# Graph attention: what the scan waits for, and the order of widening, exponentials, node maxima and compares

## The reference

```
s = einsum(Qh, Kh) / sqrt(HEAD_DIM)                 # one score for a node and head, 8 heads
alpha = leaky_relu(s[src] + s[dst], 0.2)            # edges, with a loop of each node to itself
m = segment_max(alpha, dst)
e = exp(alpha - m[dst])
a = e / segment_sum(e, dst)[dst]
attn = segment_sum(Vh[src] * a, dst)                # 256 values for a node
h = x + (attn @ Wo + bo)
```

## Time and profile before

| | |
|---|---|
| median of 3 runs | 4592.16 us (4591.9 to 4592.49) |
| the profiled execution | 4596.53 us, span 4594.5 us |
| busy share of the span: PE, DVE, ACT, POOL | 79%, 45%, 27%, 57% |
| mean granted TensorE clock | 0.891 |
| attention stage | from about 620 to 1800 us of the span |

### The profile page before, as it was taken

One profiled execution on the slowest core, in us unless ns is written; L12 is line 12 of the kernel. 1 busy time (PEld: TensorE's weight loads), 2 busy tenths in 40 slices (PEclk: granted clock), 3 DMA queues, 4 the chain that ended last, 5 costly groups with the idle time before them and its releaser, 6 DMA issues. The chain is left out here.

```text
span 4594.5 us, 70306 instructions
## 1 busy us (share of the span) xinstructions
PE 3626.4 (79%) x16651; PEld 2353.7 (51%) x16652; DVE 2077.2 (45%) x7633; ACT 1232.0 (27%) x2424; POOL 2630.5 (57%) x2830
## 2 busy tenths in 40 slices
PE   3877746666666667975999998788888888588998
PEld 1223335555555555864777776343343343367776
DVE  6976657777777775354222221222222222333332
ACT  3973322222222222254333333000000000122222
POOL 4001166666666663023666664777777777477775
PEclk9999967777777777975999999899999999799999
DMA  4431133333333331046888876777777777666675
GB/s 150 168 139 51 49 98 103 103 106 104 103 103 103 106 104 50 0 116 188 239 244 245 248 234 184 217 225 230 226 226 230 226 226 229 176 203 205 201 211 167
DMA packets 352403, 750.64 MB, mean 163 GB/s; under 512 B 82289, under 2 KB 161183, under 8 KB 348872
## 3 DMA queue, kind: packets, MB, share of 16 engines
q0 software_dynamic: 208336, 538.34, 41.3%
q10 hardware_dynamic: 72332, 112.04, 7.7%
q1 hardware_dynamic: 71529, 98.27, 6.5%
HBM read 654.57 MB, written 93.84 MB: 163 GB/s over the span
## 5 line engine op out<-in xcount | busy, mean ns | idle before, releaser
L1695 POOL DMA_INDIRECT l_gathered<-table,record x850 | 818.7, 963 | 399.5 <-issue 277.3
L780 POOL DMA_INDIRECT a_gathered<-table,record x850 | 812.3, 956 | 386.5 <-issue 263.9
L2055 POOL DMA_INDIRECT l_gathered<-table,record x850 | 814.4, 958 | 302.0 <-issue 296.2
L2149 PE MATMUL bank<-l_gathered,l_onehot 128*125 128x512 f32 x1700 | 811.2, 628 | 161.7 <-DMA l_gathered<-table,record 161.4
L2149 PEld LDWEIGHTS bank<-l_gathered,l_onehot 128*125 128x125 f32 x1700 | 325.2, 197 | 620.9 <-issue 357.4
L1110 PE MATMUL bank<-a_gathered,a_onehot 128*125 128x264 f32 x1700 | 517.9, 458 | 111.1 <-DVE a_gathered L908 111.1
L1825 ACT ACTIVATE l_part<-l_packed 128x1000 fp32r<-128x1000 bf16 (+1 forms) x300 | 314.2, 1072 | 530.1 <-PE bank L1906 427.6
L1110 PEld LDWEIGHTS bank<-a_gathered,a_onehot 128*125 128x125 f32 x1700 | 357.2, 221 | 193.1 <-DVE a_gathered L908 67.1
L1925 PE MATMUL bank<-l_gathered,l_onehot 128*125 128x256 f32 (+1 forms) x1275 | 329.3, 415 | 86.0 <-DMA l_gathered<-table,record 86.0
L2088 DVE SCALAR_TENSOR_TENSOR l_z<-l_own,one_eps,bank 125x512 f32<-125x512 f32 x50 | 37.3, 747 | 707.3 <-PE bank L2156 707.3
L1906 PE MATMUL bank<-rows_first,l_part 125*125 125x512 f32 x1250 | 307.5, 405 | 28.6 <-ACT l_part L1825 28.6
(11 more groups left out here) (265 smaller groups left out, 5042.4 us busy)
## 6 DMA issues: line engine op xcount, KB each, us to landing
l_packed<-adjacency ACTq DMA_DIRECT2D x200, 250.0 KB, 4.9
adjacency<-d_stage SPq DMA_DIRECT2D x25, 1562.5 KB
l_packed<-adjacency ACTq DMA_DIRECT2D x100, 281.2 KB, 5.8
l_gathered<-table,record POOLq DMA_INDIRECT x1700, 3.7
a_gathered<-table,record POOLq DMA_INDIRECT x850
table<-rows_first POOLq DMA_DIRECT2D x50, 250.0 KB, 3.3
table<-l_work ACTq DMA_DIRECT2D x50, 250.0 KB
l_own<-table SPq DMA_DIRECT2D x50, 250.0 KB
```

The lines of the kernel that those rows point to most:

```text
L780: pool.indirect_dma_start(out=gathered0[s][:, j * TW:(j + 1) * TW], out_offset=None, in_=table0, in_offset=bass.IndirectOffsetOnAxis(ap=re ...
L1695: pool.indirect_dma_start(out=gathered[g][:, j, :], out_offset=None, in_=table, in_offset=bass.IndirectOffsetOnAxis(ap=record[k.t][:, j, 0 ...
L2055: pool.indirect_dma_start(out=gathered[s][:, j * w:(j + 1) * w], out_offset=None, in_=table, in_offset=bass.IndirectOffsetOnAxis(ap=record ...
L2149: last = pe.matmul(sum_ps[s][0:NB, 0:w], onehot[s][:, j, :], rows[:, j, :], start=False, stop=(j == T - 1), skip_group_check=True)
```

## The change

The scan no longer waits for `prepared` but for a semaphore of its own, set by the reset row (`reset_ready`). On ACT the widening of a block's one-hot moves from the end of the round before into the block's own round, behind the self exponential. The exponential that goes to PSUM, for which DVE waits, comes first of three activations; the one that goes into the gathered rows comes second, with a semaphore (`sums_weighed`) for which PE waits ahead of quarter 0; the copy of the node maxima comes last. On DVE the next block's compares move behind the block's node maxima.

```diff
@@ vector @@
                     r = count_of(dve, rounds[s])
                     rows = gathered0[s].rearrange("p (j c) -> p j c", c=TW)
-                    dve.wait_ge(prepared[s], r)
+                    dve.wait_ge(reset_ready[s], r)
                     dve.wait_ge(rows_gathered[s], r * GATHERED)
...
                     if after is not None:
                         prepare_small(after[0], 2 * after[1] + after[0])
-                        prepare_onehot(after[0])
                     dve.wait_ge(block_begun[s], i + 1)
                     node_maxima(s, 2 * i + s, r)
+                    if after is not None:
+                        prepare_onehot(after[0])
                     if before is not None:
                         attend(before[0])
@@ scalar @@
-                    act.activation(reset[s][:, :, 1:T], rec[:, 1:T, 2].unsqueeze(1).broadcast_to([P, HEADS, T - 1]), ACT.Copy)
+                    act.activation(reset[s][:, :, 1:T], rec[:, 1:T, 2].unsqueeze(1).broadcast_to([P, HEADS, T - 1]),
+                                   ACT.Copy).then_inc(reset_ready[s], 1)
...
-                    act.activation(run_m[s][:, :], node_m[s][:, :], ACT.Copy)
-                    act.activation(rows[:, :, D:TW], alpha2[s][:, :, :], ACT.Exp)
                     act.activation(node_ps[s][:, FACTOR:FACTOR + T * HEADS].rearrange("p (j h) -> p j h", h=HEADS), alpha2[s][:, :, :],
                                    ACT.Exp).then_inc(weights_ready[s], 1)
+                    act.activation(rows[:, :, D:TW], alpha2[s][:, :, :], ACT.Exp).then_inc(sums_weighed[s], 1)
+                    act.activation(run_m[s][:, :], node_m[s][:, :], ACT.Copy)
...
                     if before is not None:
                         self_exp(*before)
+                    widen(s)
                     begin_block(s, i)
...
                     if before is not None:
                         copy_attended(*before)
-                    if after is not None:
-                        widen(after[0])
@@ tensor @@
                     if q == 0:
                         pe.wait_ge(onehot_wide[s], r)
+                        pe.wait_ge(sums_weighed[s], r)
                         pe.wait_ge(block_done[s], i + 1)
```

More of the change, by code:

```diff
@@ L667, in build @@
                                                                       pair("weights_ready"))
-            weighted, block_begun = pair("weighted"), pair("block_begun")
+            weighted, block_begun, reset_ready, sums_weighed = (pair("weighted"), pair("block_begun"), pair("reset_ready"),
+                                                               pair("sums_weighed"))
             self_loaded, self_shifted, self_weight = pair("self_loaded"), pair("self_shifted"), pair("self_weight")
@@ L1088, in _ @@
                 prepare(0)
-                widen(0)
                 over_blocks(act, first_round, more_rounds)
```

## The result

The changed kernel takes 4574.96 us (median of 6 runs, 4572.1 to 4579.97) against 4592.61 of the kernel before: a ratio of 0.996 [0.9947, 0.9973]. It is faster, as forecast, but it gains 17.6 us, where 56.6 were forecast. It lies inside the range by 1 us (the range ended at 4576), in the part that the prediction gave to the partial case of the rival "no change".

A forecast was written before the change was run, and what follows sets the result against it. Bound: a loop of waits between engines in the attention stage, none full. Gains of 48 x 0.95 + 50 x 0.32 = 61.6 us, less 5 for the clock, gave 4592.2 - 56.6 = 4536 us; range 4498 to 4576.

The forecast's parts named there:

- partial case: Slow matmuls take back part of the gain: rounds of 23.2 to 23.8 us, 4558 to 4587 us; chance 0.09.
- rival "no change": PE's slow-clock matmuls grow by as much as waits shrink: rounds stay at 23.9 us, 4592 us; chance 0.09.
- ScalarE can take the exponential where it now starts widening, at 1181.14 instead of 1183.01.: ACT's self exponential starts once widening has moved behind it; L919 on DVE then starts 1.87 us earlier.
- 0.95 earlier: DVE's scan over partitions (L854) starts 0.95 us earlier a round, at 1184.38 instead of 1185.33, in 48 rounds.
- PE's spread ... gives slack, not time: I count 0: Maxima before compares on DVE: spread ends earlier, counted 0; bounds +0.1 us (late PE selection) and -0.05 (tie at 1195.9 goes).
- The exponentials: On ACT the exponential into PSUM goes first, so DVE's weighing starts 0.32 us earlier in each of 50 rounds.
- +0.1 a round, 5 us: PE's clock shifting with new gaps: a third of rounds at -0.6 us, a sixth at +1.8.
- a sign of being wrong: First quarter on PE no longer 3.88 us in most rounds, or second quarter slow in more than a few.
- The copy L848: DVE's copy of gathered rows (formerly L847) waits for DMA instead of ScalarE, some 6.4 us into the round.
- PE as the next limit of the scan: DVE's scan is released by PE's turn of the tops, which end at 1184.34, in most rounds.
- The unequal rounds: Rounds of the attention stage become unequal, 21.9 to 24.4 us, where they were alike.
- so it fills idle time: Widening on ACT at its new place runs from about 1181.25 to 1183.2, before the residual ends at 1183.7.

The follow-up runs named there:

- Experiment 3: Changed kernel with no second rounds in ACT's program (no branch, no edge-number loads): 5872.51 us against 5942.54 for the kernel before, 0.9876, in the 6000 us condition.
- Experiment 4: Changed kernel with DVE's self shift and ACT's self exponential moved ahead of the branch, into the block's own first round: 4535.77 us against 4592.99 for the kernel before.
- experiment 5: Changed kernel with the compares back ahead of the node maxima: 4554.24 us against 4592.23 for the kernel before; 0.9953 and 0.9951 in the 6000 us condition.
- experiment 1: Kernel before with only the exponentials reordered and their new semaphore: 4580.45 us against 4592.23; 0.9976 and 0.9941 in the 6000 us condition.
- experiment 7: Changed kernel with self shift and self exponential ahead of the branch, plus 24 zero matmuls ahead of the first quarter: 4468.02 us against 4594.48 for the kernel before.
- experiments 1 to 6: The five other kernels listed here except the 4468.02 us one, plus the changed kernel with only 24 zero matmuls ahead of the first quarter (5904.79 us against 6030.07).
- experiment 2: Changed kernel with the widening back at its old place: 0.9897, 0.98 and 0.9787 of the kernel before, all in the 6000 us condition.

## Why the prediction was right and wrong

**Wrong, the step that costs the most: "ScalarE can take the exponential where it now starts widening, at 1181.14 instead of 1183.01."** The 1.87 us between those times were not all the widening's. Under it ACT's sequencer did 1.49 us of work that counts as busy nowhere, and when the widening left, that work stood bare. L920 moved from 9.42 to 9.18 into the round, not to 7.5. The scan, which was to come 0.95 earlier, comes 0.06 earlier in the mean of the rounds (11.36 against 11.42). Experiment 3 takes the pause away, and L920 stands at 7.43. Experiment 4 takes it out of the way: the scan stands at 10.47 in the mean, the 0.95 are there, and the time is 39.2 us below the changed kernel's, where 39.0 were missing.

**Wrong: "PE's spread ... gives slack, not time: I count 0", between +0.1 and -0.05.** In the condition of the result the new order of the compares costs some 20 us (experiment 5; 2 runs). The bound of +0.1 for a late selection was too small: the part behind the scan is 0.18 longer. The other 0.33 lies ahead of the scan and goes with the clock: 12 late rounds against 3. The Trainium skill ("TensorE: Matmul & The Clock Gate", section "HAM oscillation — how this bites in real kernels") says that a burst of matmuls behind a wait starts at the low clock. The rows agree for either order, since the first quarter takes 3.88 us in most rounds of both. Why more rounds stay slow beyond the first quarter is open. The long gap alone does not explain it: experiment 1 has 13 late rounds with its idle time in two gaps, and experiment 4 has 7 with it in one.

**The terms side by side,** by the medians of the runs in this condition. The exponentials gave 12 us (4592 to 4580), where 16 were forecast. The scan's semaphore and the widening gave 26 more (to 4554, experiment 5), where 48 x 0.95 = 46 were forecast. The order of the compares took 21 back (to 4575), where 0 was forecast. These runs are not all of one chip, and each has an interval of several us. The terms also do not add: undoing the pause gives 39 us and undoing the order 21, together more than the 39 that are missing.

**The clock.** "+0.1 a round, 5 us" was made of a third of the rounds at -0.6 and a sixth at +1.8. The kinds were right (most first quarters at 3.88, some rounds early at 22.7, some late near 24.5). The late ones are a quarter of the rounds and not a sixth, but each is 1.19 above the others and not 1.8: 12 x 1.19 = 14 us, where 49 / 6 x 1.8 = 15 were forecast. Only five rounds ahead of the last are below 23.0, where a third was forecast. The prediction named as a sign of being wrong that PE's second quarter is slow in more than a few rounds, and it is.

**Luck.** 5.6 of the 17.6 us lie ahead of the first weighing, where nothing was forecast. Of these, 3.4 lie between the first copy L848 (609.27, and 611.42 before) and the first weighing: there the exponential's table load no longer waits behind the copy of the maxima, and the spread runs under the compares. The other 2.2 lie ahead of any instruction that moved. The trace of the kernel before has this load, of 1.28 us, at 624.60 between the copy and the exponential, and the one of after at 614.94, in idle time. The rounds alone gave 10.5.

**Right.** The exponentials: 0.32 forecast; the idle time ahead of the weighing is 0.35 in place of 0.66, and in experiment 1 the part behind the scan is 0.30 shorter. The copy L848: it waits for DMA in 27 rounds, 6.1 into the round. PE as the next limit of the scan, at 10.47: shown by experiment 4 at 10.4. In the changed kernel PE released it in only 13 rounds. The unequal rounds, 22.7 to 24.6. That the time would not rise, and not stay where it was. The rival "no change" came in part even so: rounds of 23.57, and in experiment 1 its mechanism, slow pieces that grow while a wait shrinks (the scan 0.20 later, the part behind it 0.30 shorter).

**What the forecast should have asked.** "so it fills idle time" was asked of the widening's new place and not of its old one: what did it cover there? ACT's rows show the exponential 0.10 before the widening's end, without a gap, and that reads as if nothing lay between them. The code shows the branch at that very place.

## What to carry to other kernels

An instruction that seems to stand in the way may be the cover of work on the engine's sequencer (a branch, loads into registers) which no busy time shows; where the two neighbours of a moved instruction lie on both sides of a loop's or branch's edge, expect a gap there (here 1.4 to 1.6 us on ACT), and move the urgent instruction ahead of that edge instead. Work that is moved from ahead of a wait to behind it may have been covering that wait (here the compares covered PE's selection), and a new order that gives slack can still cost time through the clock: look at how many rounds have slow pieces behind the first burst, and not at the sum of the waits alone. And when a round is made of several terms, an experiment that makes the one assumption true (here, the exponential ahead of the branch) tells more than undoing the edit.

## What the runs showed of the hardware

Matmuls of zeros, whose result nobody reads, gave the first quarter the clock of 2.4 GHz: it takes 1.95 us in experiment 7, where it took 3.88, and the mean granted clock went from 0.900 (experiment 4) to 0.939. They do not always keep the clock up. In the round shown it fell at about 1179, stood at 0.50 from 1179.2 to 1182.4 while the fillers ran, and was back at 1.00 at 1182.8, just ahead of the quarter at 1182.99. The 24 fillers take 3.8 to 4.4 us in 20 of the 50 rounds and 2.7 in the other 30: in those 20 they take the slow stretch on themselves.

In the changed kernel DVE too sits idle for "issue" ahead of L915, its first instruction of a round, 25.7 us in 22 rounds. That this is the same work as ACT's pause at the branch is likely; no run tests it.

The 6000 us condition was met on several chips, with the kernel before and with those of experiments 1 to 6; two of these chips ran the kernel before in some 4593 us at other times. The attention stage has only a part of it: in experiment 1 its 49 rounds take 1581 us in this condition and 1161 in the other. The rest of the program was not looked at. DVE's timeline from experiment 1's first run, and PE's:

```profile
1211.81 0.42 DVE L934 TENSOR_TENSOR a_self_row<-a_self_row,a_tmp 125x256 f32<-125x256 f32 x1
1221.52 0.30 DVE L896 TENSOR_TENSOR a_alpha<-bank,a_gathered 128x136 f32<-128x136 f32 x1 [9.29 <-remote]
```

```profile
1212.83 0.17 PE L1151 MATMUL bank<-a_node_parts,a_onehotT 125*128 125x16 bf16 x1 [0.46 <-issue]
```

PE's last spread matmul begins at 1212.83, and DVE, which waits for the spread, goes on 8.7 us later. In the same trace PE pauses for "issue" 79 times ahead of spread matmuls, 54.6 us between 622 and 1790, which the trace of the kernel before never does. Nearly all rounds are 27 to 34 us long. With the maxima ahead of the compares part of that lateness lies under 2.9 us of compares and the rest of DVE's work, which may be why experiment 5 is behind experiment 2 there; no run shows it. What makes the signal late is open.
